# One small power on GpSimd behind every third indirect send of a row, in a routed network of seven stages

## The reference

```python
x = x + 0.5 * L0_ffn(layernorm(x))     # best of 8 experts per token, gelu, 128 -> 512 -> 128
x = x + L0_attn(layernorm(x))          # convolution over 4 tokens, running means of q and q*k, gelu block
x = x + 0.5 * L0_ffn(layernorm(x))     # the same experts again
x = x + 0.5 * L1_ffn(layernorm(x))     # best of 16 experts, at most 320 tokens each, relu
x = x + L1_attn(layernorm(x))          # a decaying scan over the tokens, then a layernorm
x = x + 0.5 * L1_ffn(layernorm(x))     # the 16 experts again
```

## Time and profile before

| | |
|---|---|
| time, median of 3 runs | 703.73 us (702.21 to 706.83) |
| profiled execution, first to last instruction | 768.4 us |
| mean granted TensorE clock in it | 0.918 of full speed |
| POOL busy | 367.9 us, 48%, 377 instructions |
| PE busy | 639.2 us, 83% |
| indirect sends | 128, mean 980 ns |
| indirect homes | 180 |

### The profile page before, as it was taken

The page is one execution under the profiler, slowest core; times in us unless marked ns, Lnnn a source line. Parts: engine busy times, 40 slices in busy tenths (PEclk is TensorE's granted clock), DMA queues, the critical chain, the costliest instruction groups (busy, mean ns, idle before and its releaser), DMA issues.

```text
span 768.4 us, 13116 instructions
## 1 busy us (share of the span) xinstructions
PE 639.2 (83%) x3647; PEld 490.1 (64%) x3647; DVE 449.7 (59%) x1882; ACT 329.6 (43%) x1038; POOL 367.9 (48%) x377
## 2 busy tenths in 40 slices
PE   4451799999989999857997679999997975989996
PEld 4441798986767658756986654576663764466664
DVE  6620456696899987622444330567763875166674
ACT  2220455747866544322553200645531841074551
POOL 0466346345312173554444555366661146445676
PEclk9665899999999999977999769999998997899999
DMA  9661466435103114444767212533397011455330
GB/s 302 234 176 57 124 193 197 114 93 175 61 1 81 43 41 112 140 116 130 189 206 239 69 41 67 177 97 119 110 283 158 13 37 49 116 152 169 99 98 15
DMA packets 85879, 93.95 MB, mean 122 GB/s; under 512 B 12152, under 2 KB 65307, under 8 KB 85552
## 3 DMA queue, kind: packets, MB, share of 16 engines
q1 hardware_dynamic: 73648, 74.23, 33.9%
q0 software_dynamic: 10880, 15.07, 5.9%
q10 hardware_dynamic: 1280, 3.81, 1.5%
HBM read 64.18 MB, written 33.76 MB: 127 GB/s over the span
## 4 chain that ended last, share of the span: by engine, by line
PE 52%; DVE 13%; issue 11%; POOL 7%; another core or an unknown queue 7%; DMA 5%; ACT 3%; SPq 1%; ACTq 0%; DVEq 0%; POOLq 0%
PE ps L901 8%; PE ps L921 8%; PE ps L894 8%; PE ps L821 5%; PE ps L829 5%; POOL y L1610 4%; PE ps L843 3%; PE ps L736 2%; PE ps L876 2%; PE ps L869 2%; POOL xs L1606 2%; PE ps L884 1%; PE ps L778 1%; PE ps L908 1%
## 5 line engine op out<-in xcount | busy, mean ns | idle before, releaser
L1606 POOL DMA_INDIRECT xs<-X,IDX x128 | 125.4, 980 | 143.5 <-issue 70.4
L1499 ACT ACTIVATE ht<-ps,CL 128x128 f32<-128x128 f32 x336 | 93.7, 378 | 136.1 <-PE ps L821 68.1
L1610 POOL DMA_INDIRECT y<-yt,xi x84 | 83.3, 992 | 107.3 <-DVE yt L1242 96.7
L829 PE MATMUL ps<-W,ht 128*128 (+1 forms) x672 | 94.3, 294 | 12.1 <-ACT ht L1499 8.8
L821 PE MATMUL ps<-xt,w1s 128*128 128x128 f32 x672 | 91.8, 291 | 11.4 <-DVE xt L1236 6.2
L829 PEld LDWEIGHTS ps<-W,ht 128*128 128x128 f32 x672 | 86.9, 205 | 18.8 <-issue 17.7
L821 PEld LDWEIGHTS ps<-xt,w1s 128*128 128x128 f32 x672 | 86.4, 205 | 14.0 <-DVE xt L1236 6.5
L921 PE MATMUL ps<-MT,KC 128*128 128x512 f32 x136 | 68.4, 662 | 9.6 <-remote 5.0
L1236 DVE COPY xt<-ps 128x128 f32<-128x128 f32 x84 | 24.1, 287 | 72.9 <-remote 38.4
L921 PEld LDWEIGHTS ps<-MT,KC 128*128 128x128 f32 x136 | 27.9, 212 | 43.9 <-issue 31.5
L811 PE MATMUL ps<-KC,xh 128*128 128x128 f32 x84 | 24.9, 296 | 35.0 <-issue 16.6
(11 more groups left out here) (214 smaller groups left out, 1310.9 us busy)
## 6 DMA issues: line engine op xcount, KB each, us to landing
w1s<-in_w SPq DMA_DIRECT2D x84, 256.0 KB
W<-in_w1x SPq DMA_DIRECT2D x17, 512.0 KB
wx<-in_w1x SPq DMA_DIRECT2D x15, 512.0 KB
X<-y SPq DMA_DIRECT2D x24, 256.0 KB
xs<-ZX SPq DMA_DIRECT2D x32, 185.0 KB
xi<-xs SPq DMA_DIRECT2D x84, 66.0 KB
x<-xs SPq DMA_DIRECT2D x22, 148.0 KB
X<-in_x SPq DMA_DIRECT2D x8, 264.0 KB
```

The source lines that it names most:

```text
L829: r = e.matmul(ps[TILE_BANKS[i % len(TILE_BANKS)]][:, 0:P], HT[i % NHT][:, c, :], W02[:, bass.ds(r0 * F + c * P, P)], start=(c == 0), stop ...
L1499: r = e.activation(HT[i % NHT][:, c, :], ps[TILE_BANKS[i % len(TILE_BANKS)]][:, c * P:(c + 1) * P], ACT.Gelu, bias=CL[:, bass.ds(r0 * 4 + ...
L1606: return e.indirect_dma_start(dst, bass.IndirectOffsetOnAxis(ap=IDX[:, n:n + 1], axis=0), X[:, n, 0:w], None, bounds_check=hi, oob_is_err= ...
L1610: return e.indirect_dma_start(dst, bass.IndirectOffsetOnAxis(ap=ix, axis=0), src, None, bounds_check=hi_home, oob_is_err=False, engine_sem ...
```

## The change

A step `rest` is new in POOL's table, 40 times. It raises one number of each of the 128 partitions (`EP`, the constant 1e-5) to the power -0.5 and writes it to a new tile `IDLE` that nothing reads. It waits for the memset of `EP`, and for the step before it of its kind, since both write the same tile. `rest.k` stands directly behind `send.(3k+2)` in the first layer: the steps follow `send.2`, `5`, ..., `29` (10), then `send.37`, `42`, `50`, `52`, `54`, `57`, `58`, `59`, `61` (9), then `send.64`, `67`, `68`, `71`, ..., `92` (11), then `send.98`, `101`, ..., `125` (10). In the second layer and at the start of the third, `home` steps or other powers stand in between, and there the steps are placed by the same count through the table. All steps of before keep their order on every engine; the tables of the other engines are the same and only broken into lines at other places.

```diff
+        IDLE = sb("IDLE", [P, 1])
...
             for stage, i in ORDER["pool"]:
-                if stage == "ppow":
+                if stage == "rest":
+                    POOL.wait_ge(sem("pad"), 2)
+                    if i:
+                        POOL.wait_ge(sem("rest"), i)
+                    power(IDLE[:, :], EP[:, :]).then_inc(sem("rest"), 1)
+                elif stage == "ppow":
...
     "pool": """
-send.0 send.1 send.2 send.3 send.4 send.5 send.6 send.7 send.8 send.9 send.10 send.11 send.12 send.13 send.14 send.15 send.16 send.17 send.18 send.19
...
+send.0 send.1 send.2 rest.0 send.3 send.4 send.5 rest.1 send.6 send.7 send.8 rest.2 send.9 send.10 send.11 rest.3 send.12 send.13 send.14 rest.4
+send.15 send.16 send.17 rest.5 send.18 send.19 send.20 rest.6 send.21 send.22 send.23 rest.7 send.24 send.25 send.26 rest.8 send.27 send.28 send.29
+rest.9 send.30 send.31 home.0 home.1 home.2 home.3 home.4 home.5 home.6 home.7 home.8 home.9 home.10 home.11 home.12 home.13 home.14 home.15 home.16
...
+send.38 send.39 ppow.1 send.40 send.41 send.42 rest.11 send.43 apow3.7 send.44 send.45 send.46 ppow.2 send.47 ppow.3 send.48 send.49 send.50 rest.12
+send.51 home.41 home.42 home.43 home.44 send.52 rest.13 send.53 home.45 home.46 home.47 send.54 rest.14 send.55 send.56 send.57 rest.15 home.48
+home.49 send.58 rest.16 home.50 home.51 send.59 rest.17 send.60 home.52 send.61 rest.18 send.62 send.63 home.53 home.54 home.55 home.56 home.57
...
+home.76 home.77 send.64 rest.19 send.65 send.66 send.67 rest.20 home.78 home.79 home.80 home.81 home.82 home.83 send.68 rest.21 send.69 send.70
+send.71 rest.22 send.72 send.73 send.74 rest.23 send.75 send.76 send.77 rest.24 send.78 send.79 send.80 rest.25 send.81 send.82 send.83 rest.26
+send.84 send.85 send.86 rest.27 send.87 send.88 send.89 rest.28 send.90 send.91 send.92 rest.29 send.93 send.94 send.95 epow.0 epow.1 epow.2 epow.3
...
+ehome.9 epow.14 ehome.10 ehome.11 epow.15 ehome.12 ehome.13 ehome.14 ehome.15 send.96 send.97 send.98 rest.30 send.99 send.100 send.101 rest.31
+send.102 send.103 send.104 rest.32 send.105 send.106 send.107 rest.33 send.108 send.109 send.110 rest.34 send.111 send.112 send.113 rest.35 send.114
+send.115 send.116 rest.36 send.117 send.118 send.119 rest.37 send.120 send.121 send.122 rest.38 send.123 send.124 send.125 rest.39 send.126 send.127
```

More of the change, by code:

```diff
@@ L194 @@
[L194 to L201, removed]
@@ new lines @@
+tturn.73 tup.71 tup.72 tdown.70 tturn.74 tdown.71 tdown.72 tturn.75 tup.73 tturn.76 tup.74 tup.75 tturn.77 tdown.73 tdown.74 tdown.75 pturn.14
+pturn.15 tturn.78 tup.76 pscore.16 tup.77 tdown.76 tturn.79 tup.78 tdown.77 qrank.0 tturn.80 pturn.16 tdown.78 tturn.81 tup.79 tup.80 tturn.82 tup.81
+pscore.17 tdown.79 tturn.83 tdown.80 tdown.81 tup.82 tup.83 tdown.82 qrank.1 tdown.83 pturn.17 pscore.18 pturn.18 pscore.19 qrank.2 warm.0 qrank.3
+pscore.20 warm.1 pturn.19 pturn.20 pturn.21 pscore.21 pscore.22 pscore.23 qrank.4 qrank.5 warm.2 warm.3 qrank.6 warm.4 warm.5 qrank.7 warm.6 warm.7
@@ new lines @@
+rturn.1 rB.0 rB.1 rC1.0 rC2.0 rturn.2 rturn.3 rC1.1 rB.2 rC2.1 pturn.22 pscore.24 rC1.2 rturn.4 rB.3 qrank.8 pturn.23 rC2.2 pscore.25 rC1.3 rB.4
+pturn.24 rturn.5 rC2.3 qrank.9 rC1.4 pscore.26 pturn.25 rturn.6 rB.5 qrank.10 rC2.4 pscore.27 rB.6 pturn.26 rC1.5 rC2.5 rturn.7 pscore.28 qrank.11
+rC1.6 rB.7 rC2.6 qrank.12 pturn.27 pturn.28 pscore.29 rC1.7 pscore.30 rC2.7 qrank.13 qrank.14 pturn.29 pscore.31 qrank.15 warm.50 warm.51 warm.52
+warm.53 warm.54 warm.55 warm.56 warm.57 warm.58 warm.59 warm.60 warm.61 warm.62 warm.63 warm.64 warm.65 warm.66 warm.67 eturn.16 eup.64 eup.65 eup.66
@@ L311 @@
-epow.13 ehome.9 epow.14 ehome.10 ehome.11 epow.15 ehome.12 ehome.13 ehome.14 ehome.15 send.96 send.97 send.98 send.99 send.100 send.101 send.102
-send.103 send.104 send.105 send.106 send.107 send.108 send.109 send.110 send.111 send.112 send.113 send.114 send.115 send.116 send.117 send.118
-send.119 send.120 send.121 send.122 send.123 send.124 send.125 send.126 send.127 epow.16 epow.17 epow.18 epow.19 epow.20 epow.21 ehome.16 ehome.17
-epow.22 ehome.18 epow.23 ehome.19 ehome.20 epow.24 ehome.21 epow.25 epow.26 ehome.22 epow.27 ehome.23 epow.28 ehome.24 epow.29 ehome.25 epow.30
@@ new lines @@
+agelu.9 aaff2.4 aaff2.5 agelu.10 anormA3.3 agelu.11 aaff3.3 ares.7 anormA1.7 aaff1.7 pcopy.8 anormA2.6 agelu.12 agelu.13 agelu.14 agelu.15 aaff2.6
+far.0 anormA3.4 anormA3.5 aaff3.4 anormA2.7 aaff3.5 agelu.16 agelu.17 agelu.18 agelu.19 agelu.20 aaff2.7 anormA3.6 agelu.21 pcopy.9 pcopy.10 agelu.22
+aaff3.6 agelu.23 agelu.24 agelu.25 agelu.26 agelu.27 anormA3.7 aaff3.7 agelu.28 agelu.29 agelu.30 agelu.31 pcopy.11 tgelu.41 pcopy.12 pcopy.13
+tgelu.42 tgelu.43 tgelu.44 tgelu.45 tgelu.46 tgelu.47 tgelu.48 tgelu.49 tgelu.50 tgelu.51 tgelu.52 tgelu.53 tgelu.54 tgelu.55 tgelu.56 tgelu.57
@@ new lines @@
+tgelu.58 tgelu.59 tgelu.60 tgelu.61 tgelu.62 tgelu.63 tgelu.64 tgelu.65 tgelu.66 tgelu.67 tgelu.68 tgelu.69 tgelu.70 tgelu.71 tgelu.72 tgelu.73
+tgelu.74 tgelu.75 pcopy.14 tgelu.76 tgelu.77 tgelu.78 pcopy.15 tgelu.79 tgelu.80 tgelu.81 pcopy.16 tgelu.82 tgelu.83 pcopy.17 pcopy.18 pcopy.19
+pcopy.20 pcopy.21 enorm.0 enorm.1 egexp.0 egexp.1 erela.0 erela.1 erela.2 enorm.2 enorm.3 erela.3 enorm.4 egexp.2 erela.4 erela.5 erela.6 egexp.3
+enorm.5 erela.7 erela.8 erela.9 enorm.6 egexp.4 egexp.5 erela.10 erela.11 enorm.7 egexp.6 egexp.7 erela.12 erela.13 enorm.8 erela.14 egexp.8 erela.15
@@ new lines @@
+rsq.7 rstd2.7 pcopy.29 enorm.16 enorm.17 erela.32 erela.33 enorm.18 egexp.16 egexp.17 erela.34 erela.35 enorm.19 enorm.20 egexp.18 erela.36 egexp.19
+erela.37 erela.38 egexp.20 erela.39 enorm.21 erela.40 erela.41 enorm.22 egexp.21 erela.42 erela.43 enorm.23 egexp.22 egexp.23 erela.44 erela.45
+erela.46 erela.47 enorm.24 egexp.24 enorm.25 enorm.26 erela.48 erela.49 egexp.25 egexp.26 erela.50 erela.51 enorm.27 erela.52 enorm.28 erela.53
+erela.54 egexp.27 enorm.29 erela.55 erela.56 erela.57 erela.58 enorm.30 egexp.28 erela.59 egexp.29 enorm.31 egexp.30 erela.60 erela.61 erela.62
@@ new lines @@
+home.31 home.32 home.33 home.34 home.35 home.36 apow3.0 home.37 home.38 apow3.1 home.39 home.40 apow1.2 apow1.3 apow1.4 apow1.5 apow2.2 apow1.6
+apow1.7 apow2.3 apow3.2 apow2.4 apow2.5 apow3.3 apow2.6 ppow.0 apow2.7 apow3.4 apow3.5 send.32 send.33 send.34 apow3.6 send.35 send.36 send.37 rest.10
+send.38 send.39 ppow.1 send.40 send.41 send.42 rest.11 send.43 apow3.7 send.44 send.45 send.46 ppow.2 send.47 ppow.3 send.48 send.49 send.50 rest.12
+send.51 home.41 home.42 home.43 home.44 send.52 rest.13 send.53 home.45 home.46 home.47 send.54 rest.14 send.55 send.56 send.57 rest.15 home.48
```

131 lines of the change are left out of this document (56 added, 75 removed).

## The result

The changed kernel takes 722.25 us (median, 721.31 to 723.83), the kernel before beside it on the same chip 705.28 (702.21 to 706.90): a ratio of 1.025, interval 1.0217 to 1.0283, 17 us slower.

The account below looks back on a forecast made before the run. No engine is full; POOL paces the rows of sends, and loads wait for the last send. 8 + 3 + 9 + 9 = 29 powers x 0.45 = 13 us on 703.7 gives 717 us, with 697 to 731 for 8 in 10.

Parts of the forecast that it names:

- I take 0.5 us: Duration of a one-number power on POOL, extended from the 3-number form's 0.877 us; the two slopes gave 0.58 or 0.45.
- 0.45 us for the small one: Time one small power was to add between two sends on POOL.
- Costs its duration less 0.05: Between sends on POOL, a power was to add its own duration minus 0.05 us.
- 8 + 3 + 9 + 9: Powers counted on the path in layers one to four: 29, at 0.45 us each 13 us.
- the cover of 13.3 us: Second layer: SP loads the group's first tile 13.3 us after the last send begins, against 2.4 needed for landing.
- hidden: Start of third layer: two powers near `send.64` lie ahead of homes that wait for tiles, so were to cost nothing.
- 9 of 10: Fourth layer: 9 of its 10 powers counted on the path, though 11.2 us of the row are waits for DVE.
- The recording's own cost, absent from the timed runs: Most waits without a releaser, about 54 us of the profiled chain, read as recording cost; so 13 us went on 703.7.
- Dear powers: Rival: inside a row a one-number power costs 1.17 us like one of four; 34 us, 738 us; chance 0.10.
- Covered: Rival: stalls are in the timed runs too and cover most powers in the send rows; 4 us, 708 us; chance 0.18.
- Relief: Rival: pauses in send rows let other engines' signals through, removing stalls in timed runs; placed at 680 to 697; chance 0.15.
- First use: The program's first power, moved into the first row of sends, was to cost nothing extra, against the skill's 6 us.

Follow-up runs that it names:

- f3_wide3: The changed kernel with all 40 powers raising three numbers per partition instead of one; 752.6 us, ratio 0.9805 to the kernel before on a chip where that takes 776.12.
- e1_same: The kernel before, unedited, profiled a second time; 768.49 us beside 770.81, ratio 1.0017, profiled span 767.9.
- h1_same2: The kernel before, unedited, profiled once more on another chip; 703.33 us beside 703.69, ratio 0.999, profiled span 706.0.
- f4_fill: The changed kernel with a memset of one number in place of each power; 779.36 us, ratio 1.0154 to the kernel before.
- g1_rare12: The changed kernel with 10 powers of 12 numbers each instead of 40 of one; 720.03 us beside 703.65 for the kernel before, ratio 1.0216.

## Why the prediction was right, and where it was not

**The mechanism held.** The forecast was 717 us, slower, from powers that stretch the rows of sends with nothing to hide them; measured are 722.25. The load of the last two layers still comes 2.4 us behind the last send, and the first row of 24 sends took 33.7 us where 33 were foretold. Steps in this row are 1.34, 1.27 and 1.75 us, not 1.28, 1.28 and 1.73: the transfer behind a power takes 1.03 instead of 0.97 and moves the next.

**The price of a power was too low.** "I take 0.5 us" and "0.45 us for the small one" stand against 0.60 and 0.55 (4.3 us / 8 in the first row, 4.9 / 9 in the third). The step that failed is the line drawn beyond the nearest form: from 3 numbers (0.877, and 0.905 in `f3_wide3`) to one it falls by 0.15 a number, the slope between 4 and 12, and not by the mean of the two slopes that the choice of 0.5 came to. Of the two values worked out there, 0.58 was the right one. "Costs its duration less 0.05" was right: 0.60 less 0.05.

**The count.** Foretold were 8 + 3 + 9 + 9 = 29 on the path; the table gives 14.4 us for the stretches with powers behind `send.8`, which is 26 of 0.55 us, in another split.
- First layer, 8: right (4.3 us).
- Second layer, 3 x 0.45 = 1.4 us foretold, 0.6 measured at the load. The reason was wrong: the cover of 13.3 us was mostly a stall's. Without stalls POOL waits for DVE before `send.52`, 2.31 us in before and 1.05 in after, and `send.52` comes no later than in before, counted from `send.31`: the three powers ahead of it are hidden. The six behind it put `send.63` off by 3.3 us, and the load covers 2.0 of them.
- Start of the third layer: "hidden" was wrong, `rest.19` and `rest.20` lead to 0.9 us.
- Third layer, 9: right (4.9 us).
- Fourth layer, 9 of 10: too high. The row waits for DVE before `send.100` and `send.108`, and the second of these waits, 1.72 us, is gone in after: four powers stand ahead of it and are for the most part hidden, the six behind it make 3.3 of the 3.7 us.

From the 13 us of the forecast, 29 x 0.1 = 2.9 for the price, less 3 x 0.55 = 1.7 for the count, lead to 14.3. The four stretches whose change is not the powers' (+2.8, +3.1, -2.6, -1.4) add 1.9, which is 16.2. Measured are 16.2 between the two profiles and 17.0 between the medians, so some 2 to 3 us of the loss are not traced to a power, and that the forecast lies only 5 us low owes something to a count that was too high where the price was too low.

**"The recording's own cost, absent from the timed runs" was wrong as a reason.** It put the sum on 703.7 us. The stalls were indeed absent from the runs that gave this number and from the result, but because of the chip or the occasion: on chips where they appear, the timed runs hold them (770.81 in the median, beside a profiled span of 767.9). The Trainium skill (NOTIFIC — the notification-queue block, Interfaces) says that the recording unit can hold back its producers when a buffer fills. That semaphore records are lost in just the profiles with stalls fits a crowded path for them. Whether this path is also what stops SP's moves and holds the semaphores is argued from the coincidence, not shown. A cost that only the profiled execution has is out. A cost of recording that all runs on such a chip have is not, since every timed run has its span and clock recorded too; what the kernel takes there without any recording stays open.

**The rivals.** *Dear powers* is out: 0.55, not 1.17. *Covered* is out where there are no stalls, but for the 2.0 us of the second layer; on the chips with them it is overtaken by the next. *Relief* is real, and its condition was named rightly (the stalls are "in the timed runs too"): at a ratio of 0.9847 the change gains some 12 us. If the powers cost 17 us there as elsewhere, nearly 30 us of stalls go away, an estimate. For the result itself it was false, as the profile after has none to relieve.

**First use.** The first power of after begins at 26.16, 0.10 us behind the end of its transfer, and takes 0.60 us, as the later ones do. The 6 us that the Trainium skill (GPSIMD Engine Reference, Instruction dispatch) gives for the first call to a freshly loaded kernel do not appear in this trace either. Neither trace shows whether the power's code was freshly loaded, so they do not contradict the page, as the prediction had it.

## What to carry to other kernels

Before a profile's excess over the timed runs is called the recording's cost, run the same kernel again on the chip that gave the profile: `e1_same` shows that on such a chip the timed runs are just as long. An instruction in a row that sets the pace costs its length however it is cut up, unless a wait behind it takes it up, and a cover that consists of an unexplained wait must not be counted on. A change that buys relief from a disturbance has to be timed where the disturbance is and where it is not; here it is worth -1.5% on one chip and +2.5% on another, and no form of it beat the kernel before where that takes 704 us.

## What the runs showed of the hardware

- The same kernel takes 703 to 705 us on some chips (three occasions) and 770 to 776 on others (two occasions, and the first profile's span of 768.4). The difference lies in waits whose work was done: by `send.31` `e1_same` is 3.5 us behind `h1_same2`, by `send.32` 21.0, by `send.68` 44.3, by `send.127` 62.6. What sets the chips apart is open. The granted clock is lower too (0.916 against 0.944 over the span); PE is busy for only 15.2 us more of the 61.9 (642.4 against 627.2), so the clock explains at most a part, and whether it is a cause or a consequence of PE's waits is not shown.
- On those chips plain moves of SP for tile loads take up to 700 ns, with the powers of one number too. A power behind every third send of the first row goes with a longest wait of DVE for `xt` without a releaser of 6.3 to 7.8 us (three profiles), where it is 23.2 to 30.4 without (six profiles).
- An indirect transfer behind a short instruction of POOL starts 0.18 us after it instead of 0.30 and takes 1.03 to 1.04 us instead of 0.97. A memset of 0.12 us vanishes in the gap (a step of 1.27 us in `f4_fill`).
- A power of one number over 128 partitions on GpSimd takes 0.60 us, of three 0.90 (`f3_wide3`), of twelve 2.35 (`g1_rare12`).
